# Turning the key pass's input and keys with VectorE blocks and SBUF-to-SBUF copies in place of TensorE transposes

## The chip, the cores and the metric

One Trainium2 chip, one of its NeuronCores. The metric is the device time of one execution in microseconds; the kernel before took 3483.64 us (median of three runs, 3478.65 to 3487.95).

## The reference

The input x has 8 sequences of 1024 rows of width 512. What the change touches is the first part, for the keys:

```python
xn = _layernorm(x)                       # per row, eps 1e-5, no gain
q, k, v = xn @ wq, xn @ wk, xn @ wv      # 16 heads of width 32
proj = einsum('bhsk,mk->bhsm', k * K**-0.25, omega)      # 128 features for each head
pk = exp(proj - 0.5 * sum(u * u) - max(proj)) / sqrt(128) + 1e-6
kv, z = einsum('bhsm,bhsk->bhmk', pk, v), sum(pk, axis=2)
```

Behind it stand the queries' features against kv and z, an output product, a layer norm, a feed-forward block with a second norm, and a gated block on xn shifted by a row; their sum with x is the result.

## The kernel before

The program is three passes, one behind the other. `keys_pass` (about the first 913 us of the span) normalises the rows, forms q, k and v, and sums kv and z for each sequence. `attend_pass` and `feed_forward_pass` follow; the change doesn't touch them, though the key pass's last groups already prepare the weights of the next pass.

**Tiles.** A group is 256 rows (two tiles of 128 partitions); there are 32 groups, four to a sequence. All products are in float32r with operands split in a high and a low part, three matmuls to a product. A product needs its contracted dimension on partitions, so the normalised rows `xn` must be turned (width onto partitions, `xT`), and so must the scaled keys `uk` (into `kT`). TensorE does both before the change: 8 transposes of 128x128 for `xn` (L837, jobs `turn_x` 0 and 1, four in each) and 8 for `uk` (L847, jobs `turn_k` 0 and 1), into the PSUM bank `turn`. ScalarE copies a half of the bank out as the high part (L673 `xT_hi`, L692 `kT_hi`), VectorE subtracts it from the bank for the low part (L754, L762). The same four blocks fill and empty one bank in turn.

**Order.** Each engine has a list of jobs for one round of a loop, written out by hand (`PE_BODY`, `DVE_BODY`, `ACT_BODY`, `POOL_BODY`, `SP_BODY`), with a lead: in round g, lead 2 means group g+2. Every engine works through its own list in order and waits on semaphores. TensorE's round g is: kv 0 and 1 of group g-1, `proj` 0 of group g (features of the first 128 rows), `k` 0 and 1 of g+1, kv 2, `q` 0 of g+1, `proj` 1 of g, kv 3, `q` 1, `v` 0, a `fold` (which brings a quarter of a finished sequence's kv and z into place), `v` 1, with the four turns between them. VectorE takes the maximum of a feature tile after its `proj` (`top`, L773), makes the exponent's offset (`below`, L777), takes the statistics of the next input (`stats`), the low parts of pk, the sums of kv. ScalarE copies k and its squares out of PSUM (`k`, L682 and L683), takes the exponentials (`exp`, L703), normalises x of group g+2 (`norm`, L666). SP's queue does nothing but DMAs: for each round it loads the x of g+2 (L550), stores the turned x of g+1 (L558), a finished sequence's sums (L566), the normalised rows of g+2 (L555) and the scaled queries of g+1 (L562).

**What waits for what around the turns.** `k` of a group waits for both low parts of its `xT` (semaphore `x_split`); `proj` 0 waits for both low parts of its `kT` (`k_split`); `proj` 1 also waits for the first tile's four exponentials, since it overwrites their banks. The first two groups stand in a list `HEAD`, the last two rounds in lists whose names end in `KEYS_END`, mixed with the first work of the next pass.

Of the kernel before, what the change touches and what calls it, by code (L numbers as in the profile page):

```python
# [7 lines left out]
ALU = mybir.AluOpType  # L8
# [60 lines left out]
             ("ident", "ident", 0))  # L69
# [208 lines left out]
class Norm:  # L278
# [34 lines left out]
    def invert(self, pool, g):  # L313
# [48 lines left out]
SP_KEYS_END = (("next", "w", 0, 0), ("keys", "q", 1, -1), ("next", "x", 0, 0), ("next", "mu", 0, 0),  # L362
# [5 lines left out]
def keys_pass(nc, places, shared, early, wo, w_r, w_k, w_v, mu_r, mu_k, x, wq, wk, wv, omega, xn_d, xT_d, u_d, kv_d, n_batches, groups_per_batch):  # L368
# [11 lines left out]
    with ctx:  # L380
# [3 lines left out]
        def sem(name):  # L384
            return mem.sem(name)
# [10 lines left out]
        uk = sb("uk", [P, TG, D])  # L396
        squares = [sb(f"squares{t}", [P, D]) for t in range(TG)]
# [33 lines left out]
        k_turned, k_split = sem("k_turned"), sem("k_split")  # L431
        kv_full, kv_added = sem("kv_full"), sem("kv_added")
# [52 lines left out]
        def fold_bank(g, c):  # L485
            return feat[c].t if g == G - 1 else turn if g >= G - 3 else ring[0]
# [4 lines left out]
        def rows(j):  # L491
# [51 lines left out]
        def _(sp):  # L543
# [3 lines left out]
            def do(job, n, g, b, i):  # L547
# [1582 lines left out]
```

## Time and profile before

| | us |
|---|---|
| median of three runs | 3483.64 |
| span of the profiled execution | 3482.2 |
| TensorE busy / VectorE / ScalarE / GpSimd | 3422.0 / 2468.2 / 1969.8 / 1105.2 |

The profile is of one execution, and no time beside its span is given for it; the span stands 1.4 us below the median of the runs. Busy times are of all instructions of an engine; DMA issues on SP are not counted as busy. A matmul's record lasts longer than the distance to the next one, because matmuls overlap; what a matmul costs is read from start to start.

### The profile page before, as it was taken

Reading aid. Unit: us, or ns where it says so; the run is one execution under the profiler, and the core shown is the slowest. Engines: PE = TensorE matmul, PEld = TensorE weight load, DVE = VectorE, ACT = ScalarE, POOL = GpSimd, SP = SyncE. Lnnn points to the kernel's source line nnn. Section 1 sums busy time; section 2 is a strip of 40 time slices with the busy share of each in tenths; the row PEclk is TensorE's granted clock in tenths of the full one; section 3 lists DMA queues with packets and bytes.
Section 4 is the critical chain, followed back from the end, with each engine's and each line's share of the span. In section 5 each row is a group of like instructions: output and inputs, shape, how many; then the busy total and the mean of one; then the engine's idle time right before and its main releaser. Section 6 shows DMA issues by size and latency. Waiting matters only on the chain.

```text
span 3482.2 us, 77456 instructions
## 1 busy us (share of the span) xinstructions
PE 3422.0 (98%) x29993; PEld 3151.9 (91%) x29993; DVE 2468.2 (71%) x4839; ACT 1969.8 (57%) x4240; POOL 1105.2 (32%) x861
## 2 busy tenths in 40 slices
PE   8999999999899999999999999999999999999998
PEld 6888888888788888888888889999999999999998
DVE  6767777677667777677777766666666666666666
ACT  6777777777556666666656654444444444444443
POOL 3554554545345454555555532000000000000000
PEclk9999999999899999999999999999999999999999
DMA  3222222222323333232332346444444444444443
GB/s 128 80 77 74 95 77 83 77 74 77 107 79 114 106 102 115 82 126 94 102 109 93 111 144 206 147 148 148 147 146 146 146 146 146 146 146 146 146 147 126
DMA packets 195355, 409.83 MB, mean 118 GB/s; under 512 B 27440, under 2 KB 52528, under 8 KB 194992
## 3 DMA queue, kind: packets, MB, share of 16 engines
q1 hardware_dynamic: 194992, 404.89, 34.6%
q8 instruction: 240, 3.93, 0.5%
q14 instruction: 123, 1.01, 0.1%
HBM read 292.50 MB, written 112.33 MB: 116 GB/s over the span
## 4 chain that ended last, share of the span: by engine, by line
PE 70%; DVE 2%; ACT 1%; issue 0%; POOL 0%; DMA 0%; ACTq 0%; POOLq 0%; DVEq 0%
PE ffn_hidden L175 30%; PE attend_gated L175 20%; PE ffn_result L175 8%; PE attend_num L175 6%; PE attend_feat L1425 3%; PE attend_feat L1445 1%; PE ffn_turn L1910 1%; PE attend_turn L1415 1%; DVE attend_kvz_lo L1393 1%; DVE attend_pT_lo L1354 1%; PE attend_feat L1452 1%; PE attend_turn L1434 0%; ACT attend_kvz_hi L1300 0%; DVE attend_kvz_lo L1396 0%; DMA ffn_r_in<-in_L_attn_w_dram 0%
## 5 line engine op out<-in xcount | busy, mean ns | idle before, releaser
L175 PE MATMUL ffn_hidden<-ffn_yT_hi,ffn_wa_hi 128*128 128x256 f32 x2048 | 574.1, 280 | 3.5 <-DVE ffn_wa_lo L1798 1.8
L175 PE MATMUL ffn_hidden<-ffn_yT_lo,ffn_wa_hi 128*128 128x256 f32 x2048 | 573.3, 280 | 0.0
L175 PE MATMUL ffn_hidden<-ffn_yT_hi,ffn_wa_lo 128*128 128x256 f32 x2048 | 572.0, 279 | 0.0
L316 POOL TENSOR_TENSOR ffn_n_rstd<-ffn_n_base,ffn_n_power 128x2 f32<-128x2 f32 x32 | 27.5, 860 | 1300.1 <-DVE ffn_n_negmean L311 1300.1
L1780 ACT ACTIVATE ffn_ht_hi<-ffn_hs 128x512 fp32r<-128x512 f32 x248 | 156.4, 631 | 420.6 <-DVE ffn_hs L1827 420.6
L175 PEld LDWEIGHTS ffn_hidden<-ffn_yT_hi,ffn_wa_hi 128*128 128x128 f32 x2048 | 385.0, 188 | 4.4 <-DVE ffn_wa_lo L1798 2.3
L175 PEld LDWEIGHTS ffn_hidden<-ffn_yT_hi,ffn_wa_lo 128*128 128x128 f32 x2048 | 385.2, 188 | 0.0
L175 PEld LDWEIGHTS ffn_hidden<-ffn_yT_lo,ffn_wa_hi 128*128 128x128 f32 x2048 | 384.9, 188 | 0.2
L635 POOL TENSOR_TENSOR keys_z_sum<-keys_z_sum,keys_e 128x512 f32<-128x512 f32 x192 | 259.6, 1369 | 232.9 <-ACT keys_e L703 232.9
L1831 DVE TENSOR_TENSOR ffn_ht_lo<-ffn_hs,ffn_ht_hi 128x512 fp32r<-128x512 f32 x248 | 173.6, 700 | 218.9 <-ACT ffn_ht_hi L1780 218.9
L1765 ACT ACTIVATE ffn_hid<-ffn_hidden,ffn_bias 128x256 f32<-128x256 f32 x496 | 206.1, 467 | 180.5 <-PE ffn_hidden L175 180.5
L703 ACT ACTIVATE keys_e<-keys_feat,keys_below 128x128 f32<-128x128 f32 x1024 | 283.7, 414 | 6.1 <-DVE keys_below L777 5.9
L1354 DVE SCALAR_TENSOR_TENSOR attend_pT_lo<-attend_feat,attend_pT_hi 128x512 fp32r<-128x512 f32 x256 | 163.4, 684 | 111.6 <-ACT attend_pT_hi L1225 111.2
L1335 DVE TENSOR_REDUCE attend_top<-attend_feat 128x4 f32<-128x512 f32 x256 | 159.1, 685 | 116.4 <-PE attend_feat L1425 116.3
L773 DVE TENSOR_REDUCE keys_top<-keys_feat 128x4 f32<-128x512 f32 x256 | 158.8, 683 | 114.3 <-PE keys_feat L881 114.3
L175 PE MATMUL ffn_result<-ffn_wb_lo,ffn_ht_hi 128*128 128x256 f32 x744 | 209.2, 281 | 0.0
L175 PE MATMUL ffn_result<-ffn_wb_hi,ffn_ht_lo 128*128 128x256 f32 x744 | 208.8, 281 | 0.0
L175 PE MATMUL ffn_result<-ffn_wb_hi,ffn_ht_hi 128*128 128x256 f32 x744 | 208.0, 280 | 0.0
L175 PE MATMUL ffn_hidden<-ffn_tq,ffn_ht_hi 128*128 128x256 f32 x992 | 197.8, 281 | 0.0
L783 DVE SCALAR_TENSOR_TENSOR keys_pk_lo<-keys_e,keys_pk_hi 128x512 fp32r<-128x512 f32 x256 | 185.7, 757 | 10.4 <-ACT keys_pk_hi L710 10.4
L1774 ACT ACTIVATE ffn_ht_hi<-ffn_hid 128x384 fp32r<-128x384 f32 x248 | 130.4, 526 | 107.6 <-PE ffn_result L175 102.8
L1256 ACT ACTIVATE attend_raw<-attend_num 128x512 f32<-128x512 f32 x128 | 77.0, 602 | 163.6 <-PE attend_num L175 163.6
(305 smaller groups left out, 11669.3 us busy)
## 6 DMA issues: line engine op xcount, KB each, us to landing
ffn_tq<-part_d SPq DMA_DIRECT2D x248, 512.0 KB, 3.9
keys_xin<-in_L_attn_x_dram SPq DMA_DIRECT2D x32, 512.0 KB, 4.5
xn_d<-keys_xn SPq DMA_DIRECT2D x32, 512.0 KB, 3.0
xT_d<-keys_xT_whole SPq DMA_DIRECT2D x32, 512.0 KB, 2.6
u_d<-keys_uq SPq DMA_DIRECT2D x32, 512.0 KB, 3.1
shared_xTf<-xT_d SPq DMA_DIRECT2D x32, 512.0 KB, 6.0
shared_uq<-u_d SPq DMA_DIRECT2D x32, 512.0 KB, 4.9
r_d<-shared_gate SPq DMA_DIRECT2D x32, 512.0 KB, 3.1
```

Source lines behind the costliest of these rows:

```text
L175: last = pe.matmul(out, stationary[a], moving[b], start=start and n == 0, stop=stop and n == len(TERMS) - 1)
L635: pool.tensor_tensor((z_all if last_of_batch else z_sum)[:, c, :], z_sum[:, c, :], e[t][:, c, :], ALU.add).then_inc(z_added[t], 1)
L703: last = act.activation(e[t][:, c, j * M:(j + 1) * M], feat[j].t[:, c * M:(c + 1) * M], ACT.Exp, bias=below[:, t, h:h + 1])
L773: dve.tensor_reduce(top[:, n, :, j:j + 1], feat[j].t[:, :].rearrange("p (c m) -> p c m", c=NC), AX.X, ALU.max).then_inc(top_ready, 1)
L783: dve.scalar_tensor_tensor(out=pk[t].lo[:, c, :], in0=e[t][:, c, :], scalar=FLOOR, in1=f32(pk[t].hi[:, c, :]), op0=ALU.add, op1=ALU.subtract)\
L1335: dve.tensor_reduce(top[:, n, :, j:j + 1], feat[j].t[:, :].rearrange("p (c m) -> p c m", c=NC), AX.X, ALU.max).then_inc(feat[j].free, 1)
L1354: dve.scalar_tensor_tensor(out=pT[j].lo[:, :], in0=feat[j].t[:, :], scalar=FLOOR, in1=f32(pT[j].hi[:, :]), op0=ALU.add, op1=ALU.subtract)\
L1425: last = pe.matmul(feat[j].t[:, c * M:(c + 1) * M], qT[rows(j), c, n * P:(n + 1) * P][x], omT[rows(j), :][y_], start=k == 0, stop=k == 2)
L1765: last = act.activation(hid[n % 2][:, 1 - a, :], bank.t[:, a * GT:(a + 1) * GT], ACT.Gelu, bias=bias1[:, 2 * n + a:2 * n + a + 1])
L1774: act.activation(ht[n % 2].hi[:, 0:3, :].rearrange("p q n -> p (q n)"), hid[n % 2][:, :, :].rearrange("p a n -> p (a n)")[:, 0:3 * P], ACT ...
L1780: act.activation(ht[n % 2].hi[:, 3:7, :], hs[:, :, :], ACT.Copy).then_inc(s_hi, 1)
L1831: dve.tensor_tensor(ht[n % 2].lo[:, 3:7, :], hs[:, :, :], f32(ht[n % 2].hi[:, 3:7, :]), ALU.subtract)\
```

## The change

TensorE's transposes go for all groups but the first two of x and the first of the keys. In their place, for each group:

- VectorE turns `xn` and `uk` in blocks of 32x32, two `transpose` instructions of 128x512 for each (new jobs `x_blocks` and `k_blocks`), into two new SBUF tiles. Each block is then turned in itself but stands on its old partitions.
- SP moves the blocks to their partitions with 16 SBUF-to-SBUF DMAs for each (new jobs `k_cross` and `x_cross`); a DMA moves 32 partitions by 1 KB, 32 KB. They write over `uk` and `xn`. In SP's list `k_cross` of g+1 stands behind `norm`, `x_cross` of g+2 behind `k_cross`, and the store of the queries (`q`) behind both.
- ScalarE and VectorE make the high and low parts from the moved SBUF tiles, no longer from PSUM. The jobs `turn_k` stand later in their lists than before (behind the fold and `v_out` 0), `turn_x` 0 and 1 stand together at the end.
- The fold of every group but the last goes into the bank `turn`, which has become free, and not into `ring[0]`; with it TensorE's waits at kv 0 and at the fold change.

The diff, cut to its core (the lists of the last two rounds are changed in the same way):

```diff
-             ("ident", "ident", 0))
+             ("ident", "ident", 0), ("x_blocks", "mix0_hi", 0), ("k_blocks", "mix0_lo", 0))
...
+        x_blocks, k_blocks = sb("x_blocks", [P, NC, GT]), sb("k_blocks", [P, NC, GT])
+        x_cross, k_cross = (a[:, :, :].rearrange("p t (h n) -> p (t h) n", h=2) for a in (xn, uk))
...
         def fold_bank(g, c):
-            return feat[c].t if g == G - 1 else turn if g >= G - 3 else ring[0]
+            return feat[c].t if g == G - 1 else turn
+
+        def blocks_of(blocks, t):
+
+            return blocks[:, :, :].rearrange("p j (c t s) -> p t c j s", c=NC, t=TG)[:, t]
+
+        def from_cross(cross, m):
+
+            return cross.rearrange("p i (c s) -> p c i s", s=KD)[:, 4 * m:4 * m + 4]
+
+        def in_tiles(part, m):
+
+            return part[:, 2 * m:2 * m + 2, :].rearrange("p c (t i s) -> p (c t) i s", t=TG, i=NC)
...
-        PE_BODY = [("kv", 0, -1), ("turn_x", 1, 1), ("kv", 1, -1), ("proj", 0, 0), ("k", 0, 1), ("k", 1, 1),
-                   ("kv", 2, -1), ("q", 0, 1), ("proj", 1, 0), ("turn_k", 0, 1), ("kv", 3, -1), ("q", 1, 1),
-                   ("turn_k", 1, 1), ("v", 0, 1), ("fold", 0, -1), ("turn_x", 0, 2), ("v", 1, 1)]
+        PE_BODY = [("kv", 0, -1), ("kv", 1, -1), ("proj", 0, 0), ("k", 0, 1), ("k", 1, 1), ("kv", 2, -1),
+                   ("q", 0, 1), ("proj", 1, 0), ("kv", 3, -1), ("q", 1, 1), ("v", 0, 1), ("fold", 0, -1), ("v", 1, 1)]
         DVE_BODY = [("kv", 0, -1), ("top", 0, 0), ("stats", 0, 2), ("kv", 1, -1), ("kv", 2, -1), ("top", 1, 0),
-                    ("turn_k", 0, 1), ("pk", 0, 0), ("pk", 1, 0), ("kv", 3, -1), ("turn_k", 1, 1), ("pk", 2, 0),
-                    ("pk", 3, 0), ("pk", 4, 0), ("sq", 0, 1), ("sq", 1, 1), ("v_out", 0, 1), ("pk", 5, 0),
-                    ("turn_x", 0, 2), ("pk", 6, 0), ("v_out", 1, 1), ("turn_x", 1, 2), ("pk", 7, 0)]
+                    ("k_blocks", 0, 1), ("pk", 0, 0), ("pk", 1, 0), ("kv", 3, -1), ("x_blocks", 0, 2), ("pk", 2, 0),
...
+                    ("k_blocks", 0, 1), ("pk", 0, 0), ("pk", 1, 0), ("kv", 3, -1), ("x_blocks", 0, 2), ("pk", 2, 0),
+                    ("pk", 3, 0), ("pk", 4, 0), ("sq", 0, 1), ("sq", 1, 1), ("v_out", 0, 1), ("turn_k", 0, 1),
+                    ("pk", 5, 0), ("turn_k", 1, 1), ("pk", 6, 0), ("v_out", 1, 1), ("turn_x", 0, 2), ("turn_x", 1, 2),
+                    ("pk", 7, 0)]
+                    ("v_out", 0, 1), ("fold", 0, -1), ("turn_k", 0, 1), ("hi", 5, 0), ("turn_k", 1, 1), ("exp", 6, 0),
+                    ("hi", 6, 0), ("exp", 7, 0), ("v_out", 1, 1), ("turn_x", 0, 2), ("turn_x", 1, 2), ("hi", 7, 0)]
-        SP_BODY = [("x", 0, 2), ("whole", 0, 1), ("sums", 0, -1), ("norm", 0, 2), ("q", 1, 1)]
+        SP_BODY = [("x", 0, 2), ("whole", 0, 1), ("sums", 0, -1), ("norm", 0, 2), ("k_cross", 0, 1), ("x_cross", 0, 2), ("q", 1, 1)]
...
+                if job == "k_cross":
+                    wait_alone(sp, k_blocked, g, sp_passed)
+                    for i in range(NC):
+                        for j in range(NC):
+                            sp.dma_start(k_cross[j * KD:(j + 1) * KD, i, :], k_blocks[i * KD:(i + 1) * KD, j, :])\
+                                .then_inc(k_crossed, 16)
+                if job == "x_cross":
+                    sp.wait_ge(xn_stored, 16 * g + 16)
+                    wait_alone(sp, x_blocked, g - 1, sp_passed)
+                    for i in range(NC):
+                        for j in range(NC):
+                            sp.dma_start(x_cross[j * KD:(j + 1) * KD, i, :], x_blocks[i * KD:(i + 1) * KD, j, :])\
+                                .then_inc(x_crossed, 16)
...
-                    wait(act, x_turned, 2 * g)
+                    wait(act, x_turned if g <= 2 else x_split, 2 * g)
...
+                    if g < 2:
+                        act.wait_ge(x_turned, 2 * g + n + 1)
+                        act.activation(xT[i % 2].hi[:, 2 * n:2 * n + 2, :], by_half(turn_of(g, n)), ACT.Copy)\
+                            .then_inc(xT_hi, 1)
+                    else:
+                        act.wait_ge(x_crossed, 16 * NC * NC * (g - 1))
+                        act.activation(in_tiles(xT[i % 2].hi, n), from_cross(x_cross, n), ACT.Copy).then_inc(xT_hi, 1)
...
+                    else:
+                        act.wait_ge(k_crossed, 16 * NC * NC * g)
+                        act.activation(in_tiles(kT.hi, n), from_cross(k_cross, n), ACT.Copy).then_inc(kT_hi, 1)
...
+                if job == "x_blocks":
+                    dve.wait_ge(xn_ready, TG * g + TG)
+                    wait(dve, x_crossed, 16 * NC * NC * (g - 2))
+                    for t in range(TG):
+                        last = dve.transpose(blocks_of(x_blocks, t),
+                                             xn[:, t, :].rearrange("p (c j r) -> p c j r", c=NC, j=NC))
+                    last.then_inc(x_blocked, 1)
+                if job == "k_blocks":
+                    for t in range(TG):
+                        dve.wait_ge(k_free[t], g + 1)
+                    wait(dve, k_crossed, 16 * NC * NC * (g - 1))
+                    for t in range(TG):
+                        last = dve.transpose(blocks_of(k_blocks, t),
+                                             uk[:, t, :].rearrange("p (c j r) -> p c j r", c=NC, j=NC))
+                    last.then_inc(k_blocked, 1)
...
+                    if g >= 1:
+                        dve.tensor_tensor(in_tiles(kT.lo, n), from_cross(k_cross, n), f32(in_tiles(kT.hi, n)),
+                                          ALU.subtract).then_inc(k_split, 1)
+                        return
...
-                        wait(pe, fold_out, pieces_before(min(g, G - 3)))
...
-                    if g < G - 3:
-                        pe.wait_ge(kv_added, NC * g + NC)
-                    elif g < G - 1:
-                        pe.wait_ge(k_split, min(2 * g + 6, 2 * G))
-                        if g == G - 2:
-                            pe.wait_ge(fold_out, pieces_before(g))
+                    if g < G - 1:
+                        wait(pe, fold_out, pieces_before(g))
...
```

## Rows read from the trace of the kernel before

**Rows 1.** A window of the steady key pass: length, each engine's busy time (count), granted clock, DMA share, GB/s.

```profile
440.00:850.00 410.00, 410.00 (x3513) 354.91 (x3510) 298.46 (x544) 309.85 (x825) 205.39 (x165) 1.00 0.23 81
```

**Rows 2.** TensorE's timeline over one round: start, length, line, operation, tiles, count.

```profile
439.29 0.33 PE L881 MATMUL keys_feat<-shared_omegaT_hi,keys_kT_hi 32*128 32x128 f32 x4
...
440.78 0.50 PE L175 MATMUL keys_ring<-keys_wk_hi,keys_xT_hi 128*128 128x512 f32 x1
...
455.86 0.60 PE L847 MATMUL keys_turn<-shared_ident,keys_uk 128*128 128x128 f32 x4
456.22 0.48 PE L175 MATMUL keys_ring<-keys_wv_hi,keys_xT_hi 128*128 128x512 f32 x1
456.53 0.40 PE L175 MATMUL keys_ring<-keys_wv_lo,keys_xT_hi 128*128 128x512 f32 x1
456.77 0.40 PE L175 MATMUL keys_ring<-keys_wv_hi,keys_xT_lo 128*128 128x512 f32 x1
...
466.49 0.33 PE L881 MATMUL keys_feat<-shared_omegaT_hi,keys_kT_hi 32*128 32x128 f32 x4
```

**Rows 3.** Groups of TensorE's transposes over the whole span: busy us, mean ns, idle before.

```profile
L847 PE MATMUL keys_turn<-shared_ident,keys_uk 128*128 128x128 f32 x256 | 40.2, 279 | 3.3 <-DVE keys_kT_lo L762 3.3
L837 PE MATMUL keys_turn<-shared_ident,keys_xn 128*128 128x128 f32 x252 | 38.3, 275 | 9.3 <-ACT keys_xn L666 7.7 <-DVE keys_xT_lo L754 1.7
```

**Rows 4.** VectorE's timeline in that round, with idle time before an instruction and its releaser.

```profile
451.77 2.48 DVE L773 TENSOR_REDUCE keys_top<-keys_feat 128x4 f32<-128x512 f32 x4 [3.56 <-PE keys_feat L881]
454.36 0.17 DVE L777 SCALAR_TENSOR_TENSOR keys_below<-keys_sq,keys_top 128x16 f32<-128x16 f32 x1
454.45 0.68 DVE L762 TENSOR_TENSOR keys_kT_lo<-keys_turn,keys_kT_hi 128x512 fp32r<-128x512 f32 x1
```

**Rows 5.** SP's timeline: issues of the end of the key pass's round, of small copies, and of sixteen copies.

```profile
461.81 0.43 SPq L555 DMA_DIRECT2D xn_d<-keys_xn  x1
...
1009.16 1.71 SPq L1149 DMA_DIRECT2D attend_o<-rden_d  x4
...
2119.58 0.46 SPq L1647 DMA_DIRECT2D ffn_wb_hi<-part_d  x1
...
2126.82 0.43 SPq L1647 DMA_DIRECT2D ffn_t_lo<-part_d  x1
```

**Rows 6.** Single lines of SP's queue: count, issue time min/median/max in ns, first and last start.

```profile
L1149 SPq DMA_DIRECT2D attend_o<-rden_d x128: 317/415/1646, 974.0 to 2080.9; - x128
L1134 SPq DMA_DIRECT2D den_d<-attend_raw x64: 603/637/901, 965.6 to 2070.0; - x64
```

**Rows 7.** DMA issues by line: count, KB of each, median us from issue to landing.

```profile
keys_xin<-in_L_attn_x_dram SPq DMA_DIRECT2D x32, 512.0 KB, 4.5
...
attend_o<-rden_d SPq DMA_DIRECT2D x128, 128.0 KB, 2.7
rden_d<-attend_rden SPq DMA_DIRECT2D x32, 16.0 KB, 1.4
ffn_wb_hi<-part_d SPq DMA_DIRECT2D x8, 128.0 KB, 3.7
```

**Rows 8.** ScalarE's timeline at the end of the round: the two `xT_hi` copies.

```profile
462.75 0.63 ACT L673 ACTIVATE keys_xT_hi<-keys_turn 128x512 fp32r<-128x512 f32 x1
465.71 0.60 ACT L673 ACTIVATE keys_xT_hi<-keys_turn 128x512 fp32r<-128x512 f32 x1 [0.28 <-issue]
```

**Rows 9.** Windows between the passes, columns as in rows 1 (TensorE busy first, granted clock sixth).

```profile
912.00:914.00 2.00, 0.69 (x7) 0.45 (x5) 0.45 (x1) 1.72 (x3) 0.00 (x0) 1.00 0.25 94
...
916.00:918.00 2.00, 1.05 (x29) 1.08 (x32) 0.00 (x0) 0.00 (x0) 0.81 (x6) 0.87 0.08 10
...
922.00:924.00 2.00, 2.00 (x11) 2.00 (x11) 0.92 (x3) 1.22 (x2) 0.83 (x2) 0.50 0.12 24
924.00:926.00 2.00, 0.79 (x5) 0.59 (x4) 1.61 (x3) 1.64 (x4) 2.00 (x1) 0.92 0.24 41
```

**Rows 10.** TensorE's timeline around those windows.

```profile
916.95 0.33 PE L1425 MATMUL attend_feat<-shared_omegaT_hi,shared_qT_hi 32*128 32x128 f32 x4 [4.27 <-PEq L115]
```

More of the change, by code:

```diff
@@ L318, in invert @@
         pool.tensor_tensor(self.shift[:, :], self.negmean[:, :], self.rstd[:, :], ALU.mult).then_inc(self.ready, 1)
-PE_KEYS_END = (("keys", "kv", 0, -3), ("keys", "turn_x", 1, -1), ("keys", "proj", 0, -2), ("keys", "k", 0, -1), ("keys", "kv", 1, -3),
-               ("keys", "k", 1, -1), ("keys", "q", 0, -1), ("keys", "proj", 1, -2), ("keys", "turn_k", 0, -1),
-               ("keys", "kv", 2, -3), ("keys", "kv", 3, -3), ("keys", "turn_k", 1, -1), ("keys", "q", 1, -1),
+PE_KEYS_END = (("keys", "kv", 0, -3), ("keys", "proj", 0, -2), ("keys", "k", 0, -1), ("keys", "kv", 1, -3),
+               ("keys", "k", 1, -1), ("keys", "q", 0, -1), ("keys", "proj", 1, -2),
+               ("keys", "kv", 2, -3), ("keys", "kv", 3, -3), ("keys", "q", 1, -1),
                ("keys", "v", 0, -1), ("keys", "proj", 0, -1), ("keys", "v", 1, -1), ("keys", "kv", 0, -2),
@@ L330 @@
 DVE_KEYS_END = (("keys", "top", 0, -2), ("keys", "kv", 0, -3), ("keys", "sq", 0, -1), ("keys", "kv", 1, -3),
-                ("keys", "top", 1, -2), ("keys", "turn_k", 0, -1), ("keys", "kv", 2, -3), ("keys", "sq", 1, -1),
+                ("keys", "top", 1, -2), ("keys", "kv", 2, -3), ("keys", "sq", 1, -1), ("keys", "k_blocks", 0, -1),
                 ("keys", "pk", 0, -2), ("keys", "pk", 1, -2), ("keys", "pk", 2, -2), ("next", "first", 0, 0),
-                ("keys", "kv", 3, -3), ("keys", "turn_k", 1, -1), ("keys", "pk", 3, -2), ("keys", "pk", 4, -2),
-                ("keys", "top", 0, -1), ("keys", "v_out", 0, -1), ("keys", "kv", 0, -2), ("keys", "pk", 5, -2),
+                ("keys", "kv", 3, -3), ("keys", "pk", 3, -2), ("keys", "pk", 4, -2),
+                ("keys", "turn_k", 0, -1), ("keys", "turn_k", 1, -1), ("keys", "top", 0, -1), ("keys", "v_out", 0, -1), ("keys", "kv", 0, -2), ("keys", "pk", 5, -2),
                 ("keys", "pk", 6, -2), ("keys", "pk", 7, -2), ("keys", "kv", 1, -2), ("keys", "kv", 2, -2),
@@ L361 @@
                  ("keys", "z", 7, -1), ("next", "diff", 0, 0), ("next", "mix", 0, 0))
-SP_KEYS_END = (("next", "w", 0, 0), ("keys", "q", 1, -1), ("next", "x", 0, 0), ("next", "mu", 0, 0),
+SP_KEYS_END = (("next", "w", 0, 0), ("keys", "k_cross", 0, -1), ("keys", "q", 1, -1), ("next", "x", 0, 0), ("next", "mu", 0, 0),
                ("next", "w", 1, 0), ("keys", "whole", 0, -1), ("next", "uq", 0, 0), ("next", "w", 2, 0),
@@ L505, in keys_pass @@
-                    ("v_out", 0, 1), ("fold", 0, -1), ("hi", 5, 0), ("exp", 6, 0), ("turn_x", 0, 2), ("hi", 6, 0),
-                    ("exp", 7, 0), ("v_out", 1, 1), ("turn_x", 1, 2), ("hi", 7, 0)]
+                    ("hi", 0, 0), ("norm", 0, 2), ("hi", 1, 0), ("q", 0, 1), ("hi", 2, 0),
+                    ("exp", 4, 0), ("q", 1, 1), ("hi", 3, 0), ("hi", 4, 0), ("exp", 5, 0),
+                    ("v_out", 0, 1), ("fold", 0, -1), ("turn_k", 0, 1), ("hi", 5, 0), ("turn_k", 1, 1), ("exp", 6, 0),
@@ L679, in do @@
                     act.wait_ge(k_full[n], g + 1)
-                    wait(act, k_turned, 2 * g)
+                    wait(act, k_split, 2 * g)
                     wait(act, sq_ready[n], g)
@@ L950, in do_next @@
                     last.then_inc(early.q_turned, 1)
-            run(pe, do, PE_BODY, HEAD[:-1])
+            run(pe, do, PE_BODY)
             last_groups(do, do_next, PE_KEYS_END)
```

27 lines of the change are left out of this document (16 added, 11 removed).

## The prediction

> **What bounds the kernel now.** I read the windows of the key pass first, because the change lies in it alone. In the steady stretch TensorE is busy for 410.00 of 410 us at the full granted clock, VectorE for 298.46, ScalarE for 309.85, and the DMA engines for 23% [rows 1]. The reader is to see that nothing makes TensorE wait there, so the pass is as long as TensorE's list of work, and each instruction taken from that list shortens it, as long as nothing else becomes late. Next I read TensorE's timeline for the length of a round: `proj` 0 starts at 439.29 and again at 466.49, so a round is 27.2 us [rows 2]. VectorE's timeline shows where the round turns: its maximum of the second feature tile waits 3.56 us for TensorE's `proj` 1 and starts at 451.77 [rows 4]. Last I read SP's queue, which is no busy engine in the page at all, since the change gives it 32 more DMAs a round.
>
> **What TensorE is relieved of.** 30 groups lose the 8 transposes of x and 31 groups the 8 of k: 488 of the 508 that are recorded [rows 3], in 122 blocks of four. The groups' busy time is no price, as the records overlap. From the start of a block to the start of the second matmul behind it are 456.53 - 455.86 = 0.67 us, of which a matmul of 512 columns takes 456.77 - 456.53 = 0.24 [rows 2]; a block costs 0.43 us. That is 1.7 us of a round and 122 x 0.43 = 52 us in all. If nothing were late, a round would be 25.5 us. The Trainium skill speaks of this on its page "VectorE: DVE Perf Modes" (The three transpose paths and Rules for kernel authors): 390 ns for a 128x128 transpose on TensorE, 311 ns in blocks on VectorE, and the advice to turn 128x128 on TensorE where PSUM will do as its place. An estimate from its 390 ns would be 488 x 0.39 = 190 us gained; a transpose here takes 0.11 us of the list (0.43 / 4), so the sum keeps to the row, and by the row the advice stands up.
>
> **What is added, and where it lies.** I follow one round from S, the start of `k` 0 of a group, which has to wait for the last low part of that group's turned x.
>
> 1. S to the end of `below` of `proj` 1: before it took from 440.78 to 454.36 + 0.17, 13.75 us [rows 2, 4]. TensorE has to do `k` 0, `k` 1, kv 2, `q` 0 and `proj` 1 in it, then VectorE four maxima. No turn stood in this stretch, so it stays 13.75. The statistics of the next input stand in it too; their x is now loaded behind all the copies, and takes 4.5 us to land [rows 7], but before VectorE comes to them it has to take the first four maxima, so I count that at nothing (without that cover some 2 us).
> 2. `k_blocks`, right behind `below` in VectorE's list: two instructions of 128x512. The trace has no VectorE transpose. The nearest are the maxima, 0.62 each, and the subtraction of 128x512, 0.68 [rows 4]. I take 0.65, so 1.3, and 0.1 to be seen by SP; twice that at most, and it can't be below nothing. VectorE sheds no instruction against them, yet it has over a quarter of the time free [rows 1]. `x_blocks` costs as much but lies beside SP's issues of the next step: nothing. If SP were quick it would cost 1.3.
> 3. SP issues the 16 copies of k, then the 16 of x, in that order. The trace has no SBUF-to-SBUF copy. The nearest issue is that of `attend_o`, four copies to 32 partitions each, which are 1.71 us for four [rows 5], with the gap to the next some 0.44 each. Sixteen copies of 128 partitions by 1 KB go out at (2126.82 - 2119.58) / 15 = 0.48 [rows 5]. The lowest in the long line of `attend_o` is 0.317 [rows 6], 0.36 with a gap; the dearest kind, copies of two partitions, is 0.637 [rows 6]. I take 0.45, near the row of the same partitions, and keep 0.36 and 0.64 as ends: 32 x 0.45 = 14.4 us.
> 4. The last copy lands: between 1.4 us for 16 KB and 2.7 and 3.7 for 128 KB [rows 7]; I take 2.0.
> 5. ScalarE's two copies into the high parts and VectorE's second subtraction: 0.6 + 0.6 + 0.68 and a semaphore, 2.0 [rows 4, 8]. Taken from SBUF or PSUM, I count them as equal. TensorE's `k` 0 of the next group starts.
>
> The sum is 13.75 + 1.4 + 14.4 + 2.0 + 2.0 = 33.55 us, against 27.2. It is a ring: S of one group gives S of the next, so it can't be worked off ahead. What SP had before in a round, five DMAs of some 0.4 [rows 5], lies ahead of `k_cross` or behind `x_cross` and is not in the ring. Behind the waiting `k_cross` stand `x_cross`, the store of q and the next load of x; of these `x_cross` is the one that others wait for. The copies of k themselves are in time: they land about 9.2 us before those of x, so `proj` 0 comes before S. The fold's new bank and the waits that go with it are worth nothing, since TensorE has no wait there now [rows 1]; with TensorE idle elsewhere they stay free.
>
> **TensorE's clock.** TensorE has 25.5 us of work in a round of 33.55, so it stands still for 8 us of each, mostly in the stretch ahead of S. Between the two passes it stood still 4.27 us until 916.95 [rows 10]; the granted clock then goes from 1.00 to 0.87, 0.50 and 0.92 over windows of 2 us [rows 9]. A clock of 0.5 is 1.2 GHz, 1.0 is 2.4. With the three windows between at 0.5 that is 0.5 + 6 + 0.3 = 6.8 us at half, which loses 3.4 us of work. The first 11 us behind S are on the ring, so such a fall in each round adds between 0 and 3.4 us; I take 2.5, since the idle time is longer here than there. A round is then 36.05.
>
> **The sum.** Thirty rounds: 30 x (33.55 - 27.2) = 190 us, 30 x 2.5 = 75 for the clock. In the last two rounds `proj` 0 of the last group stands only some 7.5 us of TensorE's work behind `proj` 1, where its copies need (2.8 + 1.3 + 1.4 + 7.2 + 2.0 + 2.0) = 16.7; 9 us of waiting less what the turns gave back, 7 us. The profiled execution has a span of 3482.2, 1.4 below the median of the runs, so the two can stand for each other: 3482 + 190 + 75 + 7 = 3754 us. With the low end of an issue (0.36) and no fall of the clock, 30.7 us a round and 3594; with the high end (0.64) and 3.4, 43.0 us a round and some 3960.
>
> The Trainium skill's "DMA: Bandwidth & Descriptors" (Rules for kernel authors) says to gather small transfers, as under 64 KB one pays mostly overhead, and (Anatomy of one DMA) puts the constant part near 2.0 us on the path through GpSimd. By an estimate of 2.0 us one behind another, 32 copies would be 64 us of a round and the kernel above 5000; the sixteen copies at 0.48 apart show that the parts overlap, so this has next to no chance.
>
> **Rivals.**
>
> - *The copies are cheap to issue, and it gets faster.* The ring is 19.15 + 32c us for an issue of c. It is as long as a round of now at c = 0.25 and leaves TensorE the bound at 0.20. Then 52 us are gained: 3430. For it: small copies from SBUF to SBUF with no DRAM side are not in the trace. Against it: none of 128 issues of 32 partitions was below 0.317 [rows 6].
> - *The clock holds.* The same ring without the 75 us: 3679. For it: TensorE works in two short stretches between its waits. Against it: [rows 9].
> - *Only the keys' copies are on the path*, because the x copies overlap the others more than SP's order says, or issues are near 0.3. From `proj` 0 to `below` are 454.53 - 439.29 = 15.24 [rows 2, 4], then 1.4 + 7.2 + 2.0 + 2.0 + 0.7 for a pk in between, 28.5 us: 30 x 1.3 + 7, so 3528.
> - *Issues are as dear as those of two partitions*, 0.64: 3960.
>
> **How the numbers follow.** I give the forecast 0.50, the clock that holds 0.18, the keys alone 0.12, the cheap issue 0.10, the dear one 0.10. Of these all but the cheap issue are slower by more than 0.3%, which is about what a measurement of this kernel can tell from no change; a gain or a loss inside it needs an issue within 0.24 to 0.26 us, 0.02. So faster 0.10, the same 0.02, slower 0.88. The range takes in the keys alone and ends short of the dear issue: 3520 to 3900.
>
> **What would show it.** In the changed kernel's key pass TensorE's busy share would fall to some 75%, its longest wait would be at `k` 0 on `xT_lo` and that one would name the copies behind it; SP's queue would be a row of 32 issues with no gap, about 0.45 apart; a round would be 33 to 37 us; the granted clock would drop below 1.0 in the key pass, and the later passes would be as they were. I am wrong if the issues are 0.25 us or less, or if `x_cross` is issued before `k_cross` is done.

## The result and the profile after

The changed kernel takes 3956.47 us (median of four runs, 3955.51 to 3960.74), beside it the kernel before 3481.40: a ratio of 1.136, with a 95% interval of 1.1344 to 1.1376. Slower, as forecast, but by 475 us and not by 272; the time lies above the range, at the rival with dear issues (3960). The profiled execution has a span of 3954.7 us, 472.5 above that of before. All of it is in the key pass: the first matmul of the next pass starts at 1390.6 us and not at 916.95 [rows 10], 473.6 later, and what is left of the span behind it is within 2 us of what it was.

```profile
1390.58 0.48 PE L1483 MATMUL attend_feat<-shared_omegaT_hi,shared_qT_hi 32*128 32x128 f32 x4 [4.29 <-PEq L115]
```

The windows of the key pass come first. Columns as in [rows 1]: stretch, length, busy time of TensorE, its weight loads, VectorE, ScalarE, GpSimd (counts), granted clock, DMA share, GB/s.

```profile
440.00:850.00 410.00, 282.55 (x2049) 240.72 (x2048) 221.61 (x384) 199.04 (x530) 130.87 (x107) 0.78 0.25 77
...
612.00:614.00 2.00, 0.01 (x1) 0.00 (x0) 0.00 (x0) 0.00 (x0) 0.00 (x0) 1.00 0.19 49
614.00:616.00 2.00, 0.00 (x0) 0.00 (x0) 0.00 (x0) 0.54 (x2) 0.00 (x0) 0.71 0.20 51
624.00:626.00 2.00, 0.00 (x0) 0.00 (x0) 0.00 (x0) 0.00 (x0) 0.00 (x0) 0.50 0.19 49
...
630.00:632.00 2.00, 2.00 (x7) 1.55 (x6) 2.00 (x4) 0.00 (x0) 1.59 (x1) 0.52 0.02 9
632.00:634.00 2.00, 2.00 (x10) 1.65 (x9) 1.83 (x5) 0.69 (x2) 0.00 (x0) 1.00 0.65 262
```

TensorE, busy for 410.00 of 410 us in [rows 1], is now busy for 282.55, and the others are less busy too (VectorE 221.61 for 298.46, ScalarE 199.04 for 309.85): no engine has become the bound. There are stretches of 2 us in which no engine works at all (612, 624), and the granted clock falls to 0.50 (the 1.2 GHz level) behind them; it is at 1.00 (2.4 GHz) again from 632 on, some 3 us after `k` 0 has begun at 628.82. An idle chip with a long span means a chain of waits, so TensorE's waits are next: engine and line, what it waited for, total us, times, longest.

```profile
PE keys_ring L968 <- DVE keys_pk_lo L846: 211.5, 34, 11.5
PE keys_ring L175 <- DVE keys_xT_lo L795: 154.8, 30, 5.9
...
PE keys_feat L944 <- DVE keys_kT_lo L822: 9.4, 1, 9.4
```

The second line is the wait that the prediction named, `k` 0 for `xT_lo`, once in each of 30 rounds. The first was not foreseen: kv 1 waits for pk 5, and pk 5 stands behind `turn_k` in VectorE's list, which waits for the copies of k. Both end at SP's queue. The wait of `k` 0 comes later in the round and ends last, so the way to S, the start of `k` 0, leads through it; the wait for pk 5 lies beside it. SP's timeline over one round (start, length, queue, line, copies; a wait before a row isn't shown for SP):

```profile
600.14 0.36 SPq L571 DMA_DIRECT2D xn_d<-keys_xn  x1
604.06 10.01 SPq L576 DMA_DIRECT2D keys_uk<-keys_k_blocks  x16
614.20 11.22 SPq L583 DMA_DIRECT2D keys_xn<-keys_x_blocks  x16
625.52 0.52 SPq L591 DMA_DIRECT2D u_d<-keys_uq  x1
626.09 0.47 SPq L566 DMA_DIRECT2D keys_xin<-in_L_attn_x_dram  x1
...
645.39 10.23 SPq L576 DMA_DIRECT2D keys_uk<-keys_k_blocks  x16
655.76 10.80 SPq L583 DMA_DIRECT2D keys_xn<-keys_x_blocks  x16
666.66 0.52 SPq L591 DMA_DIRECT2D u_d<-keys_uq  x1
```

Thirty-two issues stand gap to gap from 645.39 to 666.56, 21.17 us, where a whole round took 27.2 before. Round to round is 645.39 - 604.06 = 41.3. What one issue costs, and what one VectorE transpose costs, is read from the views of single lines (count, min/median/max ns, first and last start, shape):

```profile
L576 SPq DMA_DIRECT2D keys_uk<-keys_k_blocks x496: 507/591/1690, 57.4 to 1338.1; - x166
...
L583 SPq DMA_DIRECT2D keys_xn<-keys_x_blocks x480: 507/591/1797, 67.7 to 1306.6; - x160
...
L812 DVE STREAM_TRANSPOSE keys_k_blocks<-keys_uk x62: 668/686/714, 56.0 to 1327.9; 128x512 f32<-128x512 f32 x62
```

The median issue is 0.591, nearer to the 0.637 of the two-partition copies in [rows 6] than to the 0.415 of copies to 32 partitions; from start to start the 32 are 21.17 / 32 = 0.66 apart. The transpose is 0.686; 0.65 was taken between the maxima and the subtraction. The copies themselves are quick (KB each, median us from issue to landing; those of x are alike, 1.9):

```profile
keys_uk<-keys_k_blocks SPq DMA_DIRECT2D x496, 32.0 KB, 1.8
```

The rest of the ring is in the timelines of VectorE, ScalarE and TensorE, from the end of one row of issues to the start of the next (in brackets idle time and its releaser):

```profile
627.47 1.29 DVE L795 TENSOR_TENSOR keys_xT_lo<-keys_xn,keys_xT_hi 128x512 fp32r<-128x512 f32 x2 [6.35 <-ACT keys_xT_hi L708]
...
641.25 2.49 DVE L836 TENSOR_REDUCE keys_top<-keys_feat 128x4 f32<-128x512 f32 x4 [3.56 <-PE keys_feat L944]
643.84 0.17 DVE L840 SCALAR_TENSOR_TENSOR keys_below<-keys_sq,keys_top 128x16 f32<-128x16 f32 x1
643.98 1.31 DVE L812 STREAM_TRANSPOSE keys_k_blocks<-keys_uk 128x512 f32<-128x512 f32 x2
```

```profile
626.81 1.15 ACT L708 ACTIVATE keys_xT_hi<-keys_xn 128x512 fp32r<-128x512 f32 x2 [6.41 <-DMA keys_xn<-keys_x_blocks]
```

```profile
617.56 0.55 PE L968 MATMUL keys_ring<-keys_pk_hi,keys_v_parts 128*128 128x256 f32 x1 [5.55 <-DVE keys_pk_lo L846]
...
628.82 0.80 PE L175 MATMUL keys_ring<-keys_wk_hi,keys_xT_hi 128*128 128x512 f32 x1 [5.94 <-DVE keys_xT_lo L795]
629.41 0.63 PE L175 MATMUL keys_ring<-keys_wk_lo,keys_xT_hi 128*128 128x512 f32 x1
629.84 0.63 PE L175 MATMUL keys_ring<-keys_wk_hi,keys_xT_lo 128*128 128x512 f32 x1
...
1342.04 0.48 PE L944 MATMUL keys_feat<-shared_omegaT_hi,keys_kT_hi 32*128 32x128 f32 x4 [9.41 <-DVE keys_kT_lo L822]
```

So the ring closes: S is 628.82, `below` ends 15.19 later, `k_blocks` and SP's start take 1.38 to 645.39, the issues 21.17 to 666.56, the last landing until ScalarE starts 1.39 (as 625.42 to 626.81 a round earlier), the split 2.01 (626.81 to 628.82). That is 41.14.

Over the whole pass I took the distances between SP's stores of the turned x (L587). In 22 rounds they are 41.4 us apart on average; in six, every fourth from the seventh, 46.2. In the long ones another wait stands before the copies, here in three engines' timelines:

```profile
343.42 1.31 DVE L812 STREAM_TRANSPOSE keys_k_blocks<-keys_uk 128x512 f32<-128x512 f32 x2
...
349.12 0.28 ACT L756 ACTIVATE keys_kv_out<-keys_turn 128x136 f32<-128x136 f32 x1 [1.19 <-PE keys_turn L988]
...
350.41 10.39 SPq L576 DMA_DIRECT2D keys_uk<-keys_k_blocks  x16
```

`k_blocks` are ready at 344.73, but SP stands in `sums`, the store of a finished sequence, ahead of `k_cross` in its list, until ScalarE has copied the fold out at 349.40; the copies start 5.68 us late.

### The profile page after: what moved, and what is told of

It reads as the page before. It is cut to its first block, busy times and chain, and to the rows that moved or that the text cites. A ratio compares the mean times of both kernels' runs of the same rounds, so it can differ in the third digit from the quotient of the medians.

```text
span 3954.7 us, 77487 instructions
## 1 busy us (share of the span) xinstructions
PE 3498.9 (88%) x29505; PEld 3204.1 (81%) x29505; DVE 2575.6 (65%) x4961; ACT 1975.3 (50%) x4240; POOL 1095.8 (28%) x861
## 4 chain that ended last, share of the span: by engine, by line
PE 62%; DVE 2%; ACT 0%; issue 0%; POOL 0%; DMA 0%; ACTq 0%; POOLq 0%; DVEq 0%
PE ffn_hidden L175 27%; PE attend_gated L175 17%; PE ffn_result L175 7%; PE attend_num L175 5%; PE attend_feat L1483 2%; PE attend_feat L1503 1%; PE ffn_turn L1968 1%; PE attend_turn L1473 1%; DVE attend_kvz_lo L1451 1%; DVE attend_pT_lo L1412 1%; PE attend_feat L1510 0%; PE attend_turn L1492 0%; ACT attend_kvz_hi L1358 0%; DVE attend_kvz_lo L1454 0%; DMA ffn_r_in<-in_L_attn_w_dram 0%
## 5 line engine op out<-in xcount | busy, mean ns | idle before, releaser
L968 PE MATMUL keys_ring<-keys_pk_hi,keys_v_parts 128*128 128x256 f32 x512 | 154.5, 327 | 211.5 <-DVE keys_pk_lo L846 211.5
L968 PEld LDWEIGHTS keys_ring<-keys_pk_hi,keys_v_parts 128*128 128x128 f32 x512 | 111.9, 219 | 222.8 <-issue 218.3
L175 PE MATMUL keys_ring<-keys_wk_hi,keys_xT_hi 128*128 128x512 f32 x256 | 129.9, 507 | 156.3 <-DVE keys_xT_lo L795 154.8
L846 DVE SCALAR_TENSOR_TENSOR keys_pk_lo<-keys_e,keys_pk_hi 128x512 fp32r<-128x512 f32 x256 | 217.4, 879 | 26.8 <-ACT keys_pk_hi L749 26.8
```

The lines of the kernel that those rows point to most:

```text
L175: last = pe.matmul(out, stationary[a], moving[b], start=start and n == 0, stop=stop and n == len(TERMS) - 1)
L846: dve.scalar_tensor_tensor(out=pk[t].lo[:, c, :], in0=e[t][:, c, :], scalar=FLOOR, in1=f32(pk[t].hi[:, c, :]), op0=ALU.add, op1=ALU.subtract)\
L968: last = pe.matmul(kv_bank(g, n)[:, cols], v[i % 2][:, t, (2 * n + q) * P:(2 * n + q + 1) * P], pk[t][:, n, cols][s], start=t == 0 and s == 0,
```

## Experiments

My theory: the round is a ring through SP's queue, and its largest term is the time that SP takes to issue a copy, which depends on their number. Rivals: the bytes, or the DMA engines that move them, set it; the clock's fall sets it; the fold's new bank and its waits have a part in it. The median of the kernel before in the three groups of runs was 3481.74, 3483.05 and 3480.29.

**Half the bytes.** The copies take half of each row.

```diff
-   sp.dma_start(k_cross[j * KD:(j + 1) * KD, i, :], k_blocks[i * KD:(i + 1) * KD, j, :])
+   sp.dma_start(k_cross[j * KD:(j + 1) * KD, i, 0:P], k_blocks[i * KD:(i + 1) * KD, j, 0:P])
```

(the same for x)

> The same 32 copies a round, each of 32 partitions by 512 B in place of 1 KB; half of the turned values are left out, so the output is not the reference's. If the issue of a copy is what SP's queue pays, whatever it carries, the sixteen issues stay at 10.0 to 11.1 us, a round at 41 us and the time at 3956, within 15. If the DMA engines or SBUF's ports push back, the issues fall towards 0.33 us each, a round loses some 10 us and the time is near 3650.

3952.42 us, one run; SP's line:

```profile
L576 SPq DMA_DIRECT2D keys_uk<-keys_k_blocks x496: 512/591/1475, 54.6 to 1335.3; - x166
```

The median is 591 ns as before, with 16 KB and with 32 KB. The bytes are not what is paid for.

**Half the copies.**

```diff
-                        for j in range(NC):
+                        for j in range(2):
```

(in `k_cross` and `x_cross`; the counts waited for follow)

> 8 copies in place of 16 for the keys and 8 for x, each as large as before; half of the turned values are left out, so the output is not the reference's. If the ring through SP's issues sets the round, it loses 16 x 0.66 = 10.6 us of 41.4, 30 rounds give 3956 - 317 = 3640, within 30. If something beside the ring is as late (the keys' own path, the input's load), it loses less than 7 us a round and stays above 3740.

3647.0 us, one run. The issues are `x8` in 4.94 us each for k and x, and a normal round shrinks to 29.9 to 32.2 us (the long ones are 36.5 to 36.9): 16 issues fewer take 309 us off the time, 10.3 a round, 0.64 an issue. As the bytes are not, the count is what is paid for.

**The sums behind the copies.**

```diff
-   ... ("sums", 0, -1), ("norm", 0, 2), ("k_cross", 0, 1), ("x_cross", 0, 2), ("q", 1, 1)]
+   ... ("norm", 0, 2), ("k_cross", 0, 1), ("x_cross", 0, 2), ("sums", 0, -1), ("q", 1, 1)]
```

> In SP's list the store of a finished sequence's sums moves from ahead of the norm's store to behind the copies of x. If the long fourth round (46 us against 41.4) comes from the copies standing behind that store's wait for the fold, all rounds become 41.4 and 7 x 4.7 = 33 us go: 3923, within 8. If it comes from another job of a sequence's first round (the copy of z, the first sum of kv), the time stays at 3956.

3917.09 us (3916.09 and 3918.09), ratio to before 1.1247 (1.1215 to 1.128). No round is longer than 41.95 any more. The wait in `sums` cost 39 us, of which the six long rounds make 6 x (46.2 - 41.4) = 29; most of the rest is in the others, which are 41.1 on average and not 41.4.

**x from HBM.** The x copies read the same number of rows from the normalised rows in HBM, so only the source's side of the copy changes.

```diff
-   sp.dma_start(x_cross[...], x_blocks[i * KD:(i + 1) * KD, j, :])
+   sp.dma_start(x_cross[...], xn_g[g][i * KD:(i + 1) * KD, j // 2, j % 2 * GT:j % 2 * GT + GT])
```

> The 16 copies of x read 32 rows by 1 KB of the normalised input in HBM in place of the turned blocks in SBUF, to the same places; x is then not turned, so the output is not the reference's. If a copy is dear to issue because both its sides lie in SBUF, the sixteen of x fall from 10.5 us to 16 x 0.47 = 7.5 and 30 rounds lose 90 us: 3865. If it is the 32 partitions or the queue's pace whatever the source, they stay at 10 to 11 us and the time at 3956, at most 30 above for a later landing.

3892.78 us, one run: 64 us less than the changed kernel, and 28 above the expectation. The line of x:

```profile
L583 SPq DMA_DIRECT2D keys_xn<-xn_d x480: 302/421/1615, 68.9 to 1243.6; - x160
```

An issue of 32 partitions by 1 KB with HBM on one side has a median of 421 ns, as `attend_o` had with 415 [rows 6]; with SBUF on both sides it is 591. This is the row that the prediction was built on, and why it misled. HBM on one side isn't enough to make an issue cheap, though: the two-partition copies, from SBUF to HBM, have 0.637 [rows 6]. In the timeline a row of sixteen took 7.4 to 8.9 us, 7.9 on average, where it had taken 10.4 and where 16 x 0.42 is 6.7, and so the gain is smaller than the medians promise.

**k_blocks earlier.** VectorE turns k ahead of the second maxima, not behind them.

```diff
-   ... ("top", 1, 0), ("k_blocks", 0, 1), ("pk", 0, 0), ...
+   ... ("k_blocks", 0, 1), ("top", 1, 0), ("pk", 0, 0), ...
```

> In VectorE's list k_blocks moves from behind the second maxima to ahead of them, where VectorE waits 3.56 us for TensorE anyway. If the ring runs from below over k_blocks into SP's issues, the copies start some 3.5 us sooner, as the norm's store then stands ahead of them; the seven rounds in which SP waits for the sums gain nothing: 3956 - 23 x 3.5 = 3875, within 20. If the ring doesn't run through this place (the x copies wait for something else), the time stays at 3956.

3883.22 us, one run; normal rounds are 37.3 to 39.0, the long ones 45.9 to 47.7. The timelines:

```profile
604.36 1.30 DVE L812 STREAM_TRANSPOSE keys_k_blocks<-keys_uk 128x512 f32<-128x512 f32 x2 [1.90 <-ACT keys_squares L718]
...
606.71 10.32 SPq L576 DMA_DIRECT2D keys_uk<-keys_k_blocks  x16
```

The issues start earlier against S, and the ring is shorter by nearly as much: what stands ahead of SP's row is in the ring, too.

**TensorE kept busy while it waits.** Forty and 44 matmuls of 256 columns into the unused bank, ahead of kv 1 and of `k` 0.

```diff
+   if job == "fill" and g > 0:
...
+       for _ in range(n):
+           pe.matmul(turn[:, 0:GT], w["q"].hi[:, 0, 0:P], w["q"].hi[:, 1, 0:GT], start=True, stop=True)
```

> TensorE gets 40 matmuls of 256 columns into an unused bank ahead of kv 1 and 44 ahead of k 0, into the two stretches in which it waited 5.6 and 5.9 us. Nothing of the result is left out. If the fallen clock costs 1.4 us on the ring (15.2 us from k 0 to below against 13.75), the granted clock stays at 1.00 in the key pass and 30 x 1.4 = 42 us go: 3914, within 12. If the slower matmuls behind k 0 are covered by the wait, the time stays at 3956. If the filling runs at half clock it is longer than the waits and the time rises above 3990.

3953.66 us (3952.82 and 3954.5), ratio 1.1348 (1.1325 to 1.1371). The window of the whole pass:

```profile
100.00:1250.00 1150.00, 1042.83 (x8110) 938.46 (x8109) 630.82 (x1088) 562.00 (x1483) 363.76 (x298) 0.91 0.24 77
```

The mean clock rises from 0.78 to 0.91, TensorE is busy for some 240 us more of these 1150, and the time stays. One round shows why (TensorE, then VectorE):

```profile
620.08 7.33 PE L942 MATMUL keys_turn<-keys_wq_hi 128*128 128x256 f32 x44
627.25 0.40 PE L175 MATMUL keys_ring<-keys_wk_hi,keys_xT_hi 128*128 128x512 f32 x1
```

```profile
624.22 1.29 DVE L795 TENSOR_TENSOR keys_xT_lo<-keys_xn,keys_xT_hi 128x512 fp32r<-128x512 f32 x2 [5.83 <-ACT keys_xT_hi L708]
...
640.70 0.17 DVE L840 SCALAR_TENSOR_TENSOR keys_below<-keys_sq,keys_top 128x16 f32<-128x16 f32 x1
```

The clock still falls, to 0.50 from 618 to 624, and the filling runs at that level at first; from 626 on it is 1.00, so `k` 0 starts at the full clock. From S to the end of `below` are now 640.87 - 627.25 = 13.62 us, the 13.75 of before, and not 15.19. But `xT_lo` is done at 625.51, and `k` 0 stands behind the filling until 627.25, 1.74 us late. In the 14 rounds from 326 to 884 us the stretch behind S is 13.6 to 13.8 (in the changed kernel 15.1 to 16.0, 15.5 on average), and `k` 0 is 0.05 to 2.7 us late, 1.4 on average, where it was 0.06. So the fallen clock does cost the ring, some 1.8 us a round, and the filling costs nearly as much as it gives back. A filling that ends before `xT_lo` was not tried.

**The fold in its old bank.**

```diff
-   return feat[c].t if g == G - 1 else turn
+   return feat[c].t if g == G - 1 else turn if g >= G - 3 else ring[0]
```

(with the old waits at kv 0 and at the fold)

> The fold goes back into ring[0] for all but the last three groups, with the waits that belong to it at kv 0 and at the fold. If the fold's bank is worth nothing here, as TensorE waits elsewhere in each round, the time stays at 3956, within 10. If the fold in its own bank was worth a wait of 0.5 us a round, the time rises by 15.

3956.45 us, one run, the span 3954.7 as without it. The fold's move is worth nothing, as the prediction had it.

**Ten issues for thirty-two.** The blocks go to HBM in one store and come back in four loads, each 32 partitions by four rows, for k and for x; `k_blocks` stands early, the sums behind the copies, and lists of ScalarE and VectorE are put in another order.

```diff
+   if job == "k_put":
+       sp.dma_start(kb_d[g % 2], k_blocks[:, :, :]).then_inc(k_put, 16)
+   if job == "k_get":
+       sp.wait_ge(k_put, 16 * g)
+       for j in range(NC):
+           sp.dma_start(k_cross[j * KD:(j + 1) * KD, :, :],
+                        kb_d[g % 2][:, j, :].rearrange("(i r) n -> r i n", r=KD)).then_inc(k_crossed, 16)
```

(the same for x)

> The blocks go to their partitions by one store to HBM and four loads (128 partitions by 4 KB, then 32 partitions by four runs of 1 KB), 10 issues a round in place of 32, the two landings in line; k_blocks stands ahead of the second maxima, x_blocks behind them, the sums' store behind the loads, and ScalarE's and VectorE's later jobs are put in the order in which the parts come. If the number of issues in SP's queue is what made it slow, the ring is below TensorE's 25.5 us and the kernel is faster than before: 3430 to 3470. If the way through HBM or VectorE's load of 23 us a round sets the round, it is 27.5 to 30 us: 3490 to 3570.

3633.25 us (3629.97 to 3635.24, four runs), ratio 1.0428 (1.041 to 1.0445). SP's row of 21 us is gone, and with it 323 us (127 of them the two orders give without it, by the last run below), yet a round is 30.8 to 33 us and both expectations are missed. TensorE's longest line of waits is now

```profile
PE keys_ring L974 <- DVE keys_pk_lo L852: 79.7, 35, 3.3
```

and VectorE works without a gap from 497.96 to 523.39. Two readings were open: a bad order (pk 5 late), or VectorE's load.

**The same, with pk 5 early.** hi 5 and pk 5 stand ahead of `turn_k`, the squares behind `v_out` 0.

```diff
-   ... ("pk", 4, 0), ("sq", 0, 1), ("sq", 1, 1), ("turn_k", 0, 1), ("turn_k", 1, 1), ("v_out", 0, 1), ("pk", 5, 0), ...
+   ... ("pk", 4, 0), ("pk", 5, 0), ("turn_k", 0, 1), ("turn_k", 1, 1), ("v_out", 0, 1), ("sq", 0, 1), ("sq", 1, 1), ...
```

> As the kernel with one store to HBM and four loads for each of k and x, but with the high part 5 ahead of exp 6 in ScalarE's list, pk 5 ahead of turn_k, and the two squares behind v_out 0 in VectorE's. If that kernel's round of 31.4 us is held up by the late pk 5 (TensorE's kv 1 waits 2.6 us for it) and by the clock's fall behind that wait (some 3.3 us), a round becomes 25.5 to 27 us and the time 3430 to 3490. If VectorE's load, stretched while GpSimd works, sets the round, it stays at 29 to 31 us and the time is 3570 to 3630.

3593.22 us (3591.35 to 3600.17, four runs), ratio 1.0326 (1.0307 to 1.0344), rounds of 29.4 to 32.1, as the expectation has it for VectorE's load. The wait for pk falls to 6.1 us in total, but others take its place, in the steady stretch all for VectorE. No run makes VectorE's work less by itself, so that its load sets this round is read from the waits and not shown by a run. Its window, single lines (two of VectorE's subtractions), and a moment of the two engines' timelines:

```profile
440.00:850.00 410.00, 370.58 (x2937) 312.50 (x2937) 365.68 (x545) 281.34 (x759) 197.08 (x152) 0.96 0.42 142
```

```profile
L828 DVE TENSOR_TENSOR keys_kT_lo<-keys_uk,keys_kT_hi x62: 676/1755/1822, 62.2 to 976.0; 128x512 fp32r<-128x512 f32 x62
...
L801 DVE TENSOR_TENSOR keys_xT_lo<-keys_xn,keys_xT_hi x60: 673/677/694, 66.9 to 947.4; 128x512 fp32r<-128x512 f32 x60
```

```profile
517.24 5.92 POOL L670 TENSOR_TENSOR keys_z_all<-keys_z_sum,keys_e 128x512 f32<-128x512 f32 x4 [7.92 <-PE keys_turn L994]
...
517.27 3.50 DVE L828 TENSOR_TENSOR keys_kT_lo<-keys_uk,keys_kT_hi 128x512 fp32r<-128x512 f32 x2 [0.42 <-ACT keys_kT_hi L737]
```

VectorE is busy for 365.68 of 410 us, 27.2 of a round of 30.5; before it was 298.46 [rows 1], 19.8 of a round. Four transposes are 2.7 of the 7.4 more; the rest is instructions that last longer. `kT_lo` and `xT_lo` are the same subtraction of two SBUF tiles: 0.677 at a time when GpSimd is idle, 1.755 (median) beside GpSimd's sums of z. Two `kT_lo` a round make 1.3 of the 7.4 (1.35 on average in the window, for 0.69). The larger part is an instruction that the change doesn't touch, the low parts of pk, eight a round from two SBUF tiles, before and in this kernel (busy us, mean ns):

```profile
L783 DVE SCALAR_TENSOR_TENSOR keys_pk_lo<-keys_e,keys_pk_hi 128x512 fp32r<-128x512 f32 x256 | 185.7, 757 | 10.4 <-ACT keys_pk_hi L710 10.4
...
L852 DVE SCALAR_TENSOR_TENSOR keys_pk_lo<-keys_e,keys_pk_hi 128x512 fp32r<-128x512 f32 x256 | 298.0, 1212 | 0.0
```

That is 8 x (1.212 - 0.757) = 3.6 us a round; two of them, from 494.73 on, last 3.46 us together beside GpSimd's `xT_whole`, a sum of two SBUF tiles that starts at 494.88. With an operand in PSUM it was otherwise: before, two `xT_lo` that started inside GpSimd's sums of z took 0.69 each (the other at 466.34).

```profile
461.19 5.95 POOL L635 TENSOR_TENSOR keys_z_all<-keys_z_sum,keys_e 128x512 f32<-128x512 f32 x4 [9.65 <-PE keys_ring L930]
...
463.42 0.69 DVE L754 TENSOR_TENSOR keys_xT_lo<-keys_turn,keys_xT_hi 128x512 fp32r<-128x512 f32 x1 [0.38 <-ACT keys_xT_hi L673]
```

**x issued by GpSimd.** `x_cross` moves from SP's list into GpSimd's, behind z 3.

```diff
-                if job == "x_cross":                                   (sp)
-                            sp.dma_start(x_cross[...], x_blocks[...])
+                if job == "x_cross":                                   (pool)
+                            pool.dma_start(x_cross[...], x_blocks[...])
```

> The changed kernel, with the 16 copies of x issued by GpSimd's queue (behind its job z 3) and not by SP's. If what costs the time is one queue issuing 32 copies one behind another, and GpSimd issues one in some 0.6 us too, the two rows lie side by side: x_blocks end some 19 us behind S, the last x issue at 29.5, a round is 33 us and the time some 3710. If GpSimd takes 1.0 us an issue, the round is some 38.5 and the time 3880. If the copies stand in each other's way wherever they are issued (one at a time for both queues), nothing is gained: 41 us a round and 3950 or more.

3845.82 us (3845.21 to 3848.96, four runs), ratio 1.1046 (1.103 to 1.1063). The single lines, and two rows of the timelines:

```profile
L576 SPq DMA_DIRECT2D keys_uk<-keys_k_blocks x496: 508/591/1880, 57.6 to 1225.4; - x166
...
L641 POOL DMA_DIRECT2D keys_xn<-keys_x_blocks x480: 496/496/711, 60.5 to 1189.1; - x160
```

```profile
674.71 10.79 SPq L576 DMA_DIRECT2D keys_uk<-keys_k_blocks  x16
...
681.29 7.89 POOL L641 DMA_DIRECT2D keys_xn<-keys_x_blocks  x16 [12.80 <-issue]
```

The two queues issue at the same time, each at its own rate, and `xT_lo`'s wait falls from 154.8 to 6.9 us. So the time belongs to the queue that issues, not to the copies' way. The gain is less than half of what was expected: normal rounds are 36 to 40 us (the long ones 42 to 43), since the keys' chain alone is nearly as long, 37.8 of 39.65 in the round shown, and the wait for pk 5 behind it grows from 211.5 to 253.9. In 21 of the 30 rounds GpSimd begins some 0.6 us behind `x_blocks`, in six it waits for the store of the normalised rows; why it begins only at 681.29 in the round shown, when `x_blocks` were done at 677.6, stays open.

**Both orders mended.** The sums behind and `k_blocks` early, together (the two diffs above).

> The changed kernel with both orders mended at once: the store of the sums behind the copies in SP's list, and k_blocks ahead of the second maxima in VectorE's. If the two are separate terms of the sum, the gains add up: 3956 - 39 - 73 = 3844, within 15, and all rounds near 37.5 us. If the earlier copies only uncover another wait of a like size, as the kernel with k_blocks alone kept its long fourth rounds, it stays at 3870 to 3885.

3829.42 us (3825.32 to 3832.23, four runs), ratio 1.0996 (1.098 to 1.1013); all rounds are 37.2 to 38.9. The two gains add up, and somewhat more: 127 us for 39 and 73, which fits that `k_blocks` alone had left the long rounds as they were. TensorE's waits:

```profile
PE keys_ring L175 <- DVE keys_xT_lo L795: 155.2, 30, 6.1
PE keys_ring L968 <- DVE keys_pk_lo L846: 85.0, 30, 5.9
```

No order of the lists that was tried makes up for the row of issues, and no version beats the kernel before.

## Why the prediction was right in its sign and wrong in its size

- *What bounds the kernel, and where.* Right: TensorE's list before, a ring through SP's queue after; the wait of `k` 0 on `xT_lo`, the row of 32 issues without a gap and the clock below 1.0 are all in the trace, and the later passes are as they were. TensorE's longest wait is another, though, that of kv 1 for pk 5 (211.5 us for 154.8), and its busy share fell to 69% and not to 75.
- *Step 3 failed*: 32 x 0.45 = 14.4 us for SP's issues. They take 21.17. I took the row of copies over as many partitions (0.415 [rows 6]); x from HBM shows that the source's side counts: 0.421 from HBM, 0.591 from SBUF, to the same places. Half the copies and half the bytes show that it is a price for each issue. This term alone is (21.17 - 14.4) x 30 = 203 us, against 202 between forecast and time; that the two are so near is chance, since the terms below cancel each other. From start to start an issue took 0.66, a little more than the end of 0.64; I gave that rival 0.10 and cut the range short of it. That its 3960 meets the time is luck in part: its round was 43.0 us, with 3.4 for the clock, and the measured one is 41.4, with long rounds that it didn't have.
- *Steps 1, 2, 4 and 5 and the clock* come out lower together. S to `below` is 15.19 in the round taken apart, where 13.75 and 2.5 for the clock make 16.25. The clock does fall in each round, to 0.50 until some 632, so that the first `k` matmuls start some 0.43 apart and not 0.23; that loses the 1.4 us. Held at 1.00 behind S, the stretch is 13.62, so step 1 was right and the clock's term was 2.5 for a measured 1.6 in this round and some 1.8 on average. The rival in which the clock holds fell. The blocks are 1.38 for 1.4, the landing 1.39 for 2.0, the split 2.01 for 2.0. Together 1.7 us a round less than forecast: some 50 us.
- *A wait that was missed.* The prediction counted SP's other DMAs as outside the ring because they stand ahead of `k_cross`. `sums` stands there too, and it waits for the fold, which comes late in the round: 39 us by the run that moves it, 29 of them in the six long rounds. A DMA ahead of the copies is free only if what it waits for is early.
- *The end of the pass.* Right: 7 us forecast. The last `proj` 0 waits 9.41 us for `kT_lo`, where the text had 9. From the last store of a round to the last of all are 69.7 us for 48.5; a normal round in it accounts for 14.2 of the 21.2, and 7.0 are left.
- *The fold's bank* at nothing, right, by the run with the old bank. *The cheap issue* (0.25) and *only the keys' copies on the path* (28.5 us a round) fell; with x taken off SP, the keys' chain alone still makes 36 to 40 us.
- So the sum: 30 normal rounds of 41.4 for 36.05 are 160 us more, the long rounds 29, and some 13 are not accounted for, of which 5.6 stand in three early rounds that were 25.2 to 25.4 before and not 27.2.
- *The 390 and 311 ns* that the prediction takes from the Trainium skill's "VectorE: DVE Perf Modes" (The three transpose paths) stand there for bf16, and the tiles here are float32; no term of the sum rests on them.

## What to carry to other kernels

A transfer that replaces engine work has to be priced by the time its queue takes to issue it, times the number of issues, and laid against the round: 32 issues, 21 us one behind another, stood in the ring in place of the 1.7 us that TensorE had spent on its turns. Take that price from a row with the same kinds of memory on both sides, and if there is none, let the range reach the dearest row. Behind the bottleneck that is taken away, work out the next engine as well: with the issues cut to ten, VectorE was busy for 27.2 of 30.5 us, because it had four transposes more and because subtractions of two SBUF tiles, those of pk above all, now ran beside GpSimd's sums and got longer.

## What the runs showed of the hardware

- An issue on SP for 32 partitions: 0.591 us (median) with SBUF on both sides, the same for 16 KB and 32 KB, and 0.421 with HBM as its source. GpSimd issues the same SBUF copy in 0.496, beside SP. The Trainium skill, "DMA: Bandwidth & Descriptors" (Rules for kernel authors), advises to gather small transfers; half the bytes at the same time and half the count at 309 us less agree with that.
- VectorE's subtraction of two SBUF tiles takes 0.677 us alone and 1.755 (median) beside GpSimd's sums; with one operand in PSUM it took 0.69 beside them. The Trainium skill, "SBUF — State Buffer" (SBUF: two separate sides), says that a VectorE instruction with two SBUF inputs and a GpSimd instruction that reads SBUF hold their shared ports in turn, each for its whole length. The trace agrees: two subtractions that start at 517.27, with GpSimd's four sums at 517.24, take 3.50 us.
